# Score stack of a four-block kernel: twelve transfers of 32 partitions in plain channel order, the queries' high part on Pool, and a quarter of the output product moved

## What is computed

```python
src_trans = einsum('bsf,of->bso', src, W_src) + b_src      # keys and values of ctx
tgt_trans = einsum('btf,of->bto', tgt, W_tgt) + b_tgt      # queries of layernorm(x)
k, q = 8 heads of 32 channels each
scores = einsum('bthd,bshd->bhts', q, k) / sqrt(32)
scores = where(src_mask == 0, -inf, scores)
attn = softmax(scores)
tgt_update = einsum('bhts,bshd->bthd', attn, v)
out = einsum('btf,of->bto', concatenate([tgt, tgt_update]), W_out) + b_out
```

## Time and profile before

| | |
|---|---|
| median of 3 runs | 736.38 us (735.86 to 738.22) |
| the profiled execution's own time | 737.84 us |
| its span, first to last instruction | 735.4 us |
| granted TensorE clock, mean | 0.985 of full speed |
| busy: PE, ACT, DVE, POOL | 670.9, 465.6, 411.4, 198.2 us |
| stage C, first scores to last transposed scores | 282.6 to 637.1 us of the span |

### The profile page before, as it was taken

The page is one execution under the profiler, slowest core; times in us unless marked ns, Lnnn a source line. Parts: engine busy times, 40 slices in busy tenths (PEclk is TensorE's granted clock), DMA queues, the critical chain, the costliest instruction groups (busy, mean ns, idle before and its releaser), DMA issues.

```text
span 735.4 us, 11826 instructions
## 1 busy us (share of the span) xinstructions
PE 670.9 (91%) x3685; PEld 464.3 (63%) x3685; DVE 411.4 (56%) x976; ACT 465.6 (63%) x1224; POOL 198.2 (27%) x285
## 2 busy tenths in 40 slices
PE   5799999999999996889999999999999987899997
PEld 3665555545544475678777778777778775556554
DVE  7773857777755574455655545544545555335422
ACT  7566565445455523868777778777778767654453
POOL 6663433200110044131333321222221230052110
PEclk9999999999999998999999999999999998999999
DMA  8711118410000047476565676565676553001012
GB/s 286 228 64 58 58 32 253 65 58 0 1 0 1 1 54 104 74 116 91 93 93 94 97 116 91 90 92 90 100 115 89 90 65 47 2 1 58 29 58 86
DMA packets 43833, 57.78 MB, mean 79 GB/s; under 512 B 11626, under 2 KB 22284, under 8 KB 43660
## 3 DMA queue, kind: packets, MB, share of 16 engines
q1 hardware_dynamic: 43788, 57.22, 40.4%
HBM read 27.46 MB, written 4.19 MB: 43 GB/s over the span
## 4 chain that ended last, share of the span: by engine, by line
PE 56%; DMA 15%; ACT 11%; SPq 6%; DVE 6%; issue 4%; POOL 2%; ACTq 0%; DVEq 0%; POOLq 0%
DMA c_stack<-neg_row 14%; PE bank L1208 11%; ACT c_junk L979 7%; PE bank L1220 5%; SPq L524 5%; PE bank L1463 4%; PE bank L1651 4%; PE bank L1440 4%; PE bank L1184 3%; PE bank L1510 2%; PE bank L1641 2%; PE bank L1503 2%; PE bank L1188 2%; DVE c_nmx L1975 2%; PE bank L1642 2%
## 5 line engine op out<-in xcount | busy, mean ns | idle before, releaser
L979 ACT ACTIVATE c_junk<-bank,c_nmx 128x256 bf16<-128x256 f32 x256 | 116.4, 467 | 10.8 <-DVE c_nmx L1975 10.8
L1975 DVE TENSOR_REDUCE c_nmx<-bank 128x4 f32<-128x1024 f32 x64 | 75.3, 1219 | 66.4 <-PE bank L1463 66.4
L1208 PE MATMUL bank<-b_o,cw 128*128 128x512 f32 x192 | 90.8, 603 | 0.2 <-ACT b_o L831 0.2
L1463 PE MATMUL bank<-c_stack 97*128 97x256 f32 x256 | 41.3, 306 | 29.7 <-DMA c_stack<-neg_row 28.8
L1001 ACT ACTIVATE c_pT<-bank 128x1024 f32<-128x1024 f32 x64 | 63.4, 1020 | 3.6 <-PE bank L1488 2.5
L807 ACT ACTIVATE b_h<-bank,cb 128x512 f32<-128x512 f32 x48 | 32.9, 687 | 51.1 <-PE bank L1208 51.0
L1107 ACT ACTIVATE d_h<-bank,b_col 128x512 f32<-128x512 f32 x64 | 39.6, 686 | 39.3 <-PE bank L1642 39.3
L1463 PEld LDWEIGHTS bank<-c_stack 97*128 97x128 f32 x256 | 34.3, 199 | 43.2 <-issue 28.8
L1422 PE MATMUL bank<-c_ctxT,wsrcT 128*128 128x256 f32 x256 | 60.3, 379 | 0.5 <-ACT c_ctxT L955 0.5
L1208 PEld LDWEIGHTS bank<-b_o,cw 128*128 128x128 f32 x192 | 34.1, 190 | 41.3 <-issue 39.2
L1440 PE MATMUL bank<-wsrcT,c_ctxT 128*128 128x256 f32 x240 | 56.7, 379 | 0.0
(11 more groups left out here) (201 smaller groups left out, 1404.1 us busy)
## 6 DMA issues: line engine op xcount, KB each, us to landing
c_stack<-c_parts SPq DMA_DIRECT2D x96, 256.0 KB
a_ctx<-in_ctx SPq DMA_DIRECT2D x16, 512.0 KB, 3.9
c_ctx<-in_ctx SPq DMA_DIRECT2D x16, 512.0 KB, 6.9
out_x<-x_sb SPq DMA_DIRECT2D x7, 512.0 KB, 3.0
x_sb<-in_x SPq DMA_DIRECT2D x3, 1024.0 KB, 10.3
mask_b<-in_mask_BxS_fk SPq DMA_DIRECT2D x1, 2048.0 KB, 8.6
x_sb<-in_x SPq DMA_DIRECT2D x2, 512.0 KB, 4.9
wsrc_raw<-in_L_xattn_W_src SPq DMA_DIRECT2D x2, 256.0 KB, 4.1
```

What stands on the lines that cost most here:

```text
L979: op = nc.scalar.activation(c_junk[:, tc, j, :], scores(tc)[:, j, :], ACT.Exp, bias=c_nmx[hg][:, tc, j:j + 1], accum_out=c_sum[hg][:, tc, ...
L1208: op = mm(bank[2 * u + h][:], cw1[:, c, h * P:(h + 1) * P], b_o[n % LANES][:, c, :], start=c == 0, stop=c == DK - 1)
L1463: op = mm(scores(tc)[:, j, :], c_stack[s][0:MASK_ROW + 1, 0, j, hg, tc * P:(tc + 1) * P], c_stack[s][0:MASK_ROW + 1, 1, j, hg, :], start=T ...
L1975: v.tensor_reduce(c_nmx[hg][:, tc, :], scores(tc), AXIS.X, ALU.max, negate=True)\
```

## The change

The keys and queries keep plain channel order: weights and biases are loaded without `heads_mixed`, head `j` of a group is partitions `32 j` to `32 j + 31` of `c_parts`. The stack is filled by twelve transfers of 128 KB (three thirds by four heads, both sides at once), each from 32 partitions to 32. SP issues eight of them (two thirds) ahead of `rows_c(b, ..., 0)` and four behind it; every one now waits for the queries' low part too. POOL makes the queries' high part, ahead of the low one, and ACT no longer does. For the first batch the fill with ones stands behind the split of the keys. On PE `out_begin` stands ahead of the second half of the transposed scores.

```diff
-STACK_DMAS = 7
+STACK_DMAS = 3 * QH + 1
...
-            def keys_c(b, s):
+            def stack_c(b, s, thirds):
                 if b == 1:
                     sp.wait_ge(b_ok[3], 2 * PAIRS)
                 need(sp, c_k_split, 2 * b + 2)
+                need(sp, c_qlo_ok, b + 1)
                 need(sp, c_sT_ps, 2 * TS * (b - 1))
-                sides_c(b, s, 1, (K_HI, K_HI, K_LO))
-
-            def queries_c(b, s):
-                need(sp, c_qlo_ok, b + 1)
-                sides_c(b, s, 0, (Q_HI, Q_LO, Q_HI))
+                for c in thirds:
+                    first, step = ((Q_HI, K_HI - Q_HI), (Q_LO, K_HI - Q_LO), (Q_HI, K_LO - Q_HI))[c]
+                    for j in range(QH):
+                        sp.dma_start(
+                            c_stack[s][c * HD:(c + 1) * HD, :, j, :, :].rearrange("p a g t -> p a (g t)").bitcast(F32),
+                            c_parts[j * HD:(j + 1) * HD, first:first + step + 1:step, :, :]
+                            .rearrange("p a g t -> p a (g t)").bitcast(F32)).then_inc(c_stack_in, 16)
+
+            def masks_c(b, s):
...
                 if b + 1 < B:
-                    keys_c(b + 1, 1 - b % 2)
+                    stack_c(b + 1, 1 - b % 2, (0, 1))
                 rows_c(b, b % 2, 0)
                 if b + 1 < B:
-                    queries_c(b + 1, 1 - b % 2)
+                    stack_c(b + 1, 1 - b % 2, (2,))
+                    masks_c(b + 1, 1 - b % 2)
...
             def split_q(b):
+                need_alone(pool, c_q_ok, b + 1, s_passed)
+                need_alone(pool, c_stack_in, 16 * STACK_DMAS * b, s_passed)
+                nc.gpsimd.tensor_copy(c_parts[:, Q_HI, :, :], c_qT[:]).then_inc(c_qhi_ok, 1)
                 need(pool, c_qhi_ok, b + 1)
...
             split_q(0)
-            ones_c(0, c_qlo_ok, 1)
             split_k(0)
+            ones_c(0, c_k_split, 2)
...
-                high_q(b + 1)
...
                 if not first:
+                    out_begin(b - 1, 1 - s)
                     scoresT_c(b - 1, 1 - s, 1, 1)
-                    out_begin(b - 1, 1 - s)
```

More of the change, by code:

```diff
@@ L418, in row_on_all @@
             return v.partition_broadcast(P)
-        def heads_mixed(v):
-            return v.rearrange("(j d) o -> d j o", d=HD)
         loads_a = [
@@ L431, in build @@
         loads_c = [
[L432 to L434 removed]
+            (wsrc_raw[:], w_src.rearrange("(c p) f -> p c f", p=P)),
+            (wtgt_raw[:], w_tgt.rearrange("(c p) f -> p c f", p=P)),
             (wout_raw[:], w_out.rearrange("(c p) f -> p c f", p=P)),
[L436 to L439 removed]
+            (bk_col[:], column(b_src[0:D])), (bq_col[:], column(b_tgt)),
             (mask_b[:], mask.partition_broadcast(P)),
@@ L520, in stream_c @@
                 sp.dma_start(c_ctx[s][:], ctx_dram[b]).then_inc(c_ctx_in[s], 16)
-            def sides_c(b, s, side, firsts):
-                for c, part in enumerate(firsts):
-                    sp.dma_start(
-                        c_stack[s][c * HD:(c + 1) * HD, side, :, :, :].rearrange("p j g t -> p j (g t)").bitcast(F32),
-                        c_parts[:, part, :, :].rearrange("p g t -> p (g t)").bitcast(F32)).then_inc(c_stack_in, 16)
-            def keys_c(b, s):
+            def stack_c(b, s, thirds):
                 if b == 1:
@@ L551, in _ @@
             sp.wait_ge(s_neg, 1)
-            keys_c(0, 0)
-            queries_c(0, 0)
+            stack_c(0, 0, range(3))
+            masks_c(0, 0)
             stream_c(2, 0)
@@ L956, in ctxT_c @@
                                bank[src + h][:]).then_inc(c_ctxT_ok, 1)
-            def high_q(b):
-                need(act, c_q_ok, b + 1)
-                need(act, c_stack_in, 16 * STACK_DMAS * b)
-                nc.scalar.copy(c_parts[:, Q_HI, :, :], c_qT[:]).then_inc(c_qhi_ok, 1)
             def xnTq_c(b, src=5):
@@ L1086, in _ @@
             slot_b(PAIRS - 1)
-            high_q(0)
             xnT_c(0, 0)
```

7 lines of the change are left out of this document (removed).

## The result

| | before | with the change |
|---|---|---|
| median of the runs | 737.3 us (735.86 to 742.05, 4 runs) | 702.54 us (701.49 to 703.83, 4 runs) |
| the profiled execution's own time | 737.84 us | 701.87 us |
| its span | 735.4 us | 698.9 us |
| granted TensorE clock, mean | 0.985 | 0.990 |

The kernel is faster: the ratio is 0.952, with a 95% interval of 0.947 to 0.957. The forecast was 766 us and the range 728 to 792. The rival with faster transfers had 711 us at its far end, and even that was passed.

The account below looks back on a forecast made before the run. Bound: stage C's loop of stack filling, with PE and DMA engines both near their limit. New waits 16.8, clock 11.8, start 0 and batch 14 1.1 sum to 29.7 on 737.84, 767.5, median 766 us; range 728 to 792.

Parts of the forecast that it names:

- the fast rival: Stack fill in stage C: 32-to-32 transfers overlap better and get faster; 711 us at the far end; chance 0.18.
- the price of the new transfers: Stack fill: a 128 KB transfer costs between 0.62 us (issue alone) and 2.19 us; 1.10 us was taken.
- the 11.48 us to the shift rows: Stage C: shift rows usable 11.48 us after the first stack issue, 9.29 plus 2.19 for the extra data ahead.
- the wait of 3.05 in thirteen batches: PE waits 3.05 us for the shift rows before the transposed scores; batches 1 to 13 give +16.8 us.
- the clock's 11.8: Granted PE clock drops after the new waits, 1.47 us lost each time, in eight batches: +11.8 us.
- the sum: Whole kernel: 16.8 + 11.8 + 0 + 1.1 = 29.7 us on the profiled 737.84, giving 767.5, or 766 us as median.
- the upper bound: Whole kernel: 775 us, the upper end of 752 to 775 from the bounds of clock and stage start.
- break-even: Stack fill: below 1.85 us for 256 KB (142 GB/s) shift rows come by 368.0 and the kernel is no slower.
- The costly rival: Stack fill: twelve small transfers cost more than six, 0.1 to 0.3 us fixed part each; 776 to 797 us; chance 0.15.
- First scores: Start of stage C: PE's first scores row was forecast near 280.2.
- The moved quarter: PE in stage C: 0.86 us of output product moved earlier; transposed scores end 0.50 later, PE 0.36 further on afterwards.
- The high part on POOL: Queries' split: ACT gains 0.6 us a batch, worth nothing while not the bound; POOL 1.3 us later would delay the stack.

Follow-up runs that it names:

- Kernel 1: The changed kernel with the old transfers put back: mixed channel order, six of 256 KB, four ahead of the shift rows and two behind; 763.86 us, ratio 1.036.

## Why the prediction was wrong

- **The step that failed is the price of the new transfers**: "I take half of that, 1.10, the same rate, because the target of 32 partitions stays as it is, and the engines are busy with bytes." It measured 0.64, the lower bound that stood in the same sentence (0.62, the issue alone). Busy engines said nothing of what they were busy with: with the source as wide as the target the same bytes take the engines 0.88 of the time at 206 GB/s instead of 1.06 at 122. The reason that I gave against the fast rival, same target and same bytes, was a guess about a resource that no row showed. From this step follow the 11.48 us to the shift rows, the wait of 3.05 in thirteen batches (0.9 us in all were measured) and the clock's 11.8.
- **What was built on it held up.** Kernel 1 has the new order with the old transfers and takes 763.9 us, 26.6 more than the kernel before on that chip, where the sum had 29.7: the wait for the shift rows (2.0 to 2.8 for 3.05) and the clock are both there. So the sum was roughly right for a kernel that has the old price. Two slips in it are small: the upper bound adds up to 773 and not 775 (736.4 + 16.8 + 17.6 + 1.3 + 1.1), and the batch of 21.96 that it starts from is shorter than the mean of the thirteen, 22.21.
- **The fast rival is what happened**, though not by all of its reason. That reading over 128 partitions against writing 32 was the cost is borne out, though by the span and not by the number (32 partitions at spacing 4 are as slow). Its "since half of them read other partitions than are written" is not: the six transfers of 256 KB that read the very partitions they write are as fast. Its break-even was 1.85 us for 256 KB; measured are 1.28. Its far end had 20.2 us a batch; measured are 20.06. The Trainium skill (SBUF — State Buffer, Door 1: the DMA port swizzle) had 189 GB/s for 32 partitions; by that figure this rival would win, and the trace now shows 206 for 32 to 32. It had a chance of 0.18, which was too little when the only thing against it was that guess. The range left out its better half, and the measured time lies beyond even that half's far end.
- **711 was still 8.5 us too high.** Thirteen batches at 20.06 are 1.8 of them; the start gave 5.9 instead of 2.4 (3.94 at the first scores and 1.95 in batch 0), with the 0.54 from before the stage in it; batch 14 gave 2.8 that the rival had left out.
- **The costly rival** had a part of each transfer that doesn't shrink with its size. None shows: 128 KB take 0.64 us and 256 KB 1.32 from neighbouring partitions.
- **First scores** at 278.68 instead of the forecast 280.2 (with the fill at the old price). The queries' new wait costs nothing, as forecast: POOL ends both parts at 345.23, before SP can start at 346.25.
- **The moved quarter** was forecast to put PE 0.36 us further on in a batch; undoing it costs 5.8 us, 0.39 in each of 15. **The high part on POOL** was taken as worth nothing beside the bound, and it is 14.5 us if ACT keeps it. The prediction saw that a later low part would delay the whole stack, and did not put a price on the copy's old place.
- **What I had not looked at** is POOL's fill beside DVE. At 264.55 to 268.06 it now lies, with the addition that follows, beside DVE's b_tt, which takes 3.20 us instead of 1.92, and PE's stall behind it is 2.14 instead of 0.86; the clock falls after it. The 1.92 before was not undisturbed either: POOL split the keys then, and the same pair takes 0.73 where POOL is idle. Without the fill the start might have gained 1.3 us more, an estimate from the two stalls; no run took the fill away.

POOL's fill and DVE's pair with the change, then the pair before:

```profile
264.55 3.51 POOL L707 MEMSET c_stack<- 3x4096 f32 x1
...
266.36 3.20 DVE L1822 TENSOR_SCALAR b_tt<-b_tt,k_tt,b_kb 128x256 f32<-128x256 f32 x2
...
272.73 0.73 DVE L1822 TENSOR_SCALAR b_tt<-b_tt,k_tt,b_kb 128x256 f32<-128x256 f32 x2
```

```profile
266.89 1.92 DVE L1833 TENSOR_SCALAR b_tt<-b_tt,k_tt,b_kb 128x256 f32<-128x256 f32 x2
```

The start of stage C with the change, windows with PEclk, and PE's rows with the two stalls ahead of them:

```profile
273.00:276.00 3.00, 3.00 (x12) 2.61 (x11) 2.93 (x6) 0.76 (x2) 0.00 (x0) 0.52 0.70 225
289.50:292.50 3.00, 2.75 (x9) 1.97 (x10) 2.69 (x4) 2.75 (x10) 0.00 (x0) 0.50 0.88 208
```

```profile
272.27 1.83 PE L1277 MATMUL bank<-ident,b_o 128*128 128x128 f32 x8 [2.14 <-DVE b_o L1829]
...
289.43 1.01 PE L1403 MATMUL bank<-ident,c_ctx 128*128 128x128 f32 x4 [2.10 <-DVE c_vb L1956]
```

After each of these idle times the granted clock was at its lower level, 1.2 GHz, for some 3 us, as the prediction had read it from the 2.18 us wait before. It doesn't follow every such wait: in kernel 1 it stayed up after waits of 2.76, 2.34 and 2.36 us. Without long waits in the batches it stays up there, and the mean rose from 0.985 to 0.990.

## What to carry to other kernels

A DMA engine that is busy throughout is not thereby busy with bytes: look at GB/s beside the share, and if the rate is far below another row's, treat the shape of the transfer as an unknown with both ends open. When a change alters that shape and the sign hangs on it, give the ends of the bounds their chances, and don't take a middle for want of a row. When rearranging channels between partitions within SBUF, try the layout in which each transfer's source spans no more partitions than its target of 32, even at the price of twice as many transfers, as long as the issuing queue keeps up. And a part that seems free (the high part on POOL) can be what another part needs (the common wait): undo them one by one.

## What the runs showed of the hardware that I had not expected

- Copies within SBUF: 122 GB/s from 128 partitions to 32, 156 from 64 to 32, 153 from every second of 64 to 32, 123 from every fourth of 128 to 32, and 206, limited by the issue, from 32 in a row to 32. Into 16 partitions: 150 from 16, 128 from 32, 122 from 64.
- A DMA issue on SP took 0.64 us for 128 KB and for 256 KB, even where each of these landed only 2.14 us after the one before. In the run with six quick transfers of 256 KB the fourth to sixth issue took 1.34 to 1.36 us each, about the pace of the landings (1.32 on average). Why those, and not the issues of the slow transfers, no run shows.
- DVE beside POOL: two instructions that take 0.73 us with POOL idle took 1.92 beside its split of the keys and 3.20 beside a 3.51 us fill and the addition behind it, and a cast of 0.17 us took 2.04 and ended with POOL's fill.
